# Five of six attentions make their probabilities with keys on partitions

## The reference

```python
# L0: three residual parts
x += attn(ln(x), ln(x), causal, 16 heads, rotary q and k)      # "L0s", 128 keys
x += attn(ln(x), ctx, 16 heads, rotary q and k)                # "L0c", 77 keys
x += gelu(ln(x) @ fc1 + b) @ fc2 + b
# L1
x += attn(ln(x), ln(x), 16 heads)                              # "L1s", 128 keys
x += attn(ln(x), ln(ctx), 16 heads)                            # "L1c", 77 keys
x += top-2 of 8 experts, each 128 -> 512 -> 128
# L2
x += mamba2 block(x)
x += attn(ln(x), ctx, 8 heads, mask over keys)                 # "L2c", 77 keys
# L3
x = ln(x + attn(x, ctx, 16 heads, mask over query-key pairs))  # "L3c", 77 keys
# every attention: softmax(q k^T / sqrt(width)) v, then @ wo
```

## Time and profile before

| what | value |
|---|---|
| median of 3 runs | 3726.12 us (3721.3 to 3736.9) |
| the profiled execution's own time | 3734.74 us |
| its span, first to last instruction | 3732.9 us |
| PE busy | 3195.7 us, 86% |
| ACT busy | 2652.3 us, 71% |
| DVE busy | 2605.4 us, 70% |
| POOL busy | 1246.9 us, 33% |
| mean granted clock of TensorE | 0.952 of full speed |

### The profile page before, as it was taken

One profiled execution on the slowest core, in us unless ns is written; L12 is line 12 of the kernel. 1 busy time (PEld: TensorE's weight loads), 2 busy tenths in 40 slices (PEclk: granted clock), 3 DMA queues, 4 the chain that ended last, 5 costly groups with the idle time before them and its releaser, 6 DMA issues.

```text
span 3732.9 us, 87645 instructions
## 1 busy us (share of the span) xinstructions
PE 3195.7 (86%) x30064; PEld 2269.6 (61%) x30064; DVE 2605.4 (70%) x5408; ACT 2652.3 (71%) x5088; POOL 1246.9 (33%) x1615
## 2 busy tenths in 40 slices
PE   6898888888888979998988888998888997777897
PEld 3566556566756657665665656666565665665565
DVE  7877787755477777556888777665888877326775
ACT  4777777777876757887776766788776776656566
POOL 3122333212153353112244244212235434214632
PEclk9999999999999989999999999999999998989899
DMA  7013200134410033221000014322000004442000
GB/s 280 1 43 135 109 6 15 30 97 108 103 37 3 18 100 89 69 64 43 19 22 14 3 44 109 83 72 57 26 23 20 6 19 108 103 112 59 16 2 13
DMA packets 211920, 212.98 MB, mean 57 GB/s; under 512 B 51808, under 2 KB 155168, under 8 KB 211232
## 3 DMA queue, kind: packets, MB, share of 16 engines
q1 hardware_dynamic: 203296, 190.58, 18.1%
q0 software_dynamic: 8192, 16.79, 1.5%
HBM read 135.98 MB, written 71.30 MB: 56 GB/s over the span
## 4 chain that ended last, share of the span: by engine, by line
PE 39%; DVE 23%; ACT 15%; issue 8%; SPq 7%; DMA 4%; POOL 4%; ACTq 0%; DVEq 0%; POOLq 0%
PE ps L1933 8%; DVE mx L2320 6%; PE ps L1923 5%; PE ps L1945 4%; DVE pr L2326 4%; DMA b_up<-cols 4%; ACT block_hid L2211 3%; ACT pt L2164 3%; PE ps L1892 3%; PE ps L1953 2%; PE ps L2005 2%; PE ps L1918 2%; DVE kx L2326 2%; ACT xh L2114 2%; SPq L1818 1%
## 5 line engine op out<-in xcount | busy, mean ns | idle before, releaser
L2320 DVE TENSOR_REDUCE mx<-ps 128x8 f32<-128x616 f32 (+1 forms) x704 | 671.4, 954 | 334.7 <-PE ps L1923 316.4
L2164 ACT ACTIVATE pt<-ps 77x512 f32<-77x512 f32 (+1 forms) x1408 | 768.9, 593 | 126.1 <-PE ps L1933 123.2
L2576 POOL TENSOR_TENSOR kx<-kT,in_tiles 128x308 f32<-128x308 f32 (+1 forms) x384 | 315.7, 822 | 830.5 <-PE ps L1923 740.0
L1933 PE MATMUL ps<-k_sb,pr 128*77 128x128 f32 (+1 forms) x3776 | 538.9, 284 | 33.9 <-ACT pr L2155 10.3
L1933 PEld LDWEIGHTS ps<-k_sb,pr 128*77 128x77 f32 (+1 forms) x3776 | 421.1, 147 | 142.2 <-issue 73.2
L1945 PE MATMUL ps<-pt,v 77*16 77x128 f32 (+2 forms) x11264 | 444.3, 278 | 29.0 <-ACT pt L2164 11.2
L2326 DVE TENSOR_TENSOR pr<-ps,mx 128x616 f32<-128x616 f32 (+1 forms) x472 | 450.3, 954 | 16.2
L2155 ACT ACTIVATE pr<-pr 128x616 f32<-128x616 f32 (+1 forms) x472 | 392.7, 840 | 75.6 <-DVE pr L2326 74.6
L2173 ACT ACTIVATE og<-ps 128x256 f32<-128x256 f32 x704 | 267.3, 381 | 236.8 <-PE ps L1945 233.6
L1923 PE MATMUL ps<-kx,qT 32*128 32x308 f32 (+2 forms) x2816 | 361.6, 547 | 42.2 <-ACT pt L2164 15.8
L1945 PEld LDWEIGHTS ps<-pt,v 77*16 77x16 f32 (+2 forms) x11264 | 251.8, 97 | 181.1 <-issue 85.1
(11 more groups left out here) (209 smaller groups left out, 5733.3 us busy)
## 6 DMA issues: line engine op xcount, KB each, us to landing
w_up<-weights SPq DMA_DIRECT2D x160, 256.0 KB
w_down<-weights SPq DMA_DIRECT2D x160, 256.0 KB
sent<-block_hid SPq DMA_DIRECT2D x42, 512.0 KB, 6.3
made<-block_hid SPq DMA_DIRECT2D x42, 512.0 KB, 6.3
block_rows<-sent SPq DMA_DIRECT2D x160, 64.0 KB
b_down<-expert_b SPq DMA_DIRECT2D x160, 64.0 KB
made<-block_out SPq DMA_DIRECT2D x160, 64.0 KB, 2.2
cT<-ctx_cols SPq DMA_DIRECT2D x32, 154.0 KB, 3.1
```

Of the source, the lines that this page charges most:

```text
L1933: i = tr(p[0:keys, j * L:(j + 1) * L], probs[s][pl.slot(unit, 3)][:, c:c + keys], ident)
L2164: go_act(pt[s][0:keys, q % 2, :], p[0:keys, :], ACT.Copy).then_inc(probsT_ready.sem, 1)
L2320: link(v_.tensor_reduce(m, tile, AX.X, ALU.max, negate=True))
L2576: tell(pool, g_.tensor_tensor(spread_keys[s][:, pl.slot(step, 2), 0:4 * keys].rearrange("p (h k) -> p h k", h=4), kT[s][:, b * keys:(b + 1 ...
```

## The change

Attentions 0 to 4 (all but L3c) are made another way, called flipped; those with 16 heads and 77 keys (L0c and L1c) are moreover flat. L3c stays as it was.

- `scores` stays, mask included, but now only for the maximum: `peak` is the DVE reduction alone. The addition from PSUM to SBUF, the exponential over it, the transposes of `turn` and their ACT copies are gone.
- `split` (POOL, four small instructions) writes the negated maxima as a sum of three bfloat16 numbers into `pieces`, 32 columns to a group of four heads. `shift` (PE, then a DVE copy) turns that into rows on partitions with one bfloat16 matmul.
- `scores_t` (PE) makes the scores again, transposed: the spread keys are stationary, 128 (or the keys of one head) columns at a time, the queries move. Per block of 128 queries and per row group there is one float32 matmul, and one bfloat16 matmul of a constant times the shift rows adds the maximum. For 128 keys that is four blocks x four row groups x two matmuls; for flat, the 4 x 77 = 308 keys of four heads are cut into three chunks of 128 rows, so three blocks; for the 8-head attention four blocks x two row groups. The causal mask is added again by four bfloat16 matmuls of 512 columns.
- `exp` (ACT) takes the exponential straight from two PSUM banks into SBUF, keys already on partitions: 1024 columns, or 768 for flat. The key mask of L2c is the bias of this instruction.
- `mix` is as before for 128 keys and for the 8 heads, without the wait for a copy. For flat it takes three chunks x four groups of heads, with values laid out in rows of the chunks, and ACT copies 384 columns once instead of 256 twice. `regroup` then turns three blocks instead of four and takes six DVE instructions instead of two, as heads cut by a chunk's edge come in two parts.
- Flat values need `blank` (ACT, two instructions that lay zeros and ones) and `chunk` (SP, six small transfers from the values to their rows), once per pass and attention. A third buffer for spread keys.
- `rope` has one projection into one bank, and four DVE instructions (the swap of halves is a shuffle across partitions).
- Costs, priorities and so the order of all steps on all engines are new.

```diff
+        self.flat = flip and heads == 16 and keys == LC
+        self.spreads = 3 if flip else 2
+        self.pitch = 4 * keys if self.flat else 4 * L
...
+              "L0_sa_bo", rope=True, mask="causal", norm=0, flip=True),
...
+    Attention("L2c", 8, LC, "L2_wq", "L2_wk", "L2_wv", "L2_wo", mask="keys", norm=8, flip=True),
...
+    if t.flat:
+        values = [("blank", a, s)] + values + [("chunk", a, s)]
...
+def flipped_steps(a, s):
+
+    t = ATT[a]
+    out = [("spread", a, s, 0)]
+    turned = t.halves - 1 if t.flat else 0
+    for n in range(NB + 2):
+        if n < NB:
+            out.append(("scores", a, s, n))
+            if n + 1 < NB:
+                out.append(("spread", a, s, n + 1))
+            out += [("peak", a, s, n, h) for h in range(t.halves)]
+        if 1 <= n <= NB:
+            out.append(("shift", a, s, n - 1))
+        if n < NB:
+            out.append(("split", a, s, n))
+        if n >= 3:
+            out.append(("regroup", a, s, n - 3))
+        if n >= 2:
+            out.append(("mix", a, s, n - 2, turned))
+        if 1 <= n <= NB:
+            out.append(("scores_t", a, s, n - 1))
+            out += [("exp", a, s, n - 1, h) for h in range(t.halves)]
+        if n >= 2 and t.halves == 2 and not t.flat:
+            out.append(("mix", a, s, n - 2, 1))
+    return out
...
+def last_use(a, s, b):
+
+    t = ATT[a]
+    if b >= t.spreads:
+        return ("scores_t" if t.flip else "scores", a, s, b - t.spreads)
+    return ("mix", a - 1, s, NB - 1, ATT[a - 1].halves - 1)
...
-    return TWO if step[0] == "rope" else ONE if step[0] in WITH_PSUM else None
+    return ONE if step[0] in WITH_PSUM else None
...
+        flipped = Ring([(pr[s][:, 0, :], pr[s][:, 1, :], flat_pt[s]) for s in range(S)])
...
+        def probs_by_key(s, t, slot):
+
+            if t.flat and slot < 2:
+                return flat_pr[s][:, slot * 6 * L:(slot + 1) * 6 * L]
+            return flipped[s][slot][:, 0:(6 if t.flat else 8) * L]
...
+                elif kind == "chunk":
+
+                    a, s = step[1:]
+                    sp.wait_ge(*blanked(a, s))
+                    sp.wait_ge(*values_ready(a, s))
+                    for c in range(3):
+                        for slot, (j, key, row, n) in enumerate(pieces_of_chunk(c)):
+                            sp.dma_start(value_rows(s, c)[row:row + n, slot * ROW:slot * ROW + 128],
+                                         flat_v1[s][key:key + n, j * 128:(j + 1) * 128]).then_inc(chunks_in[s], 16)
...
-                    if t.rope:
-                        i = mm(bank(pl, step, 1)[:, 0:n], W(w + "r"), src[:, 0:n], start=True, stop=True)
...
+                elif kind == "shift":
+
+                    a, s, b = args
+                    pe.wait_ge(*peaks_split(a, s, b))
+                    mm(p[:, 0:L], pieces[:, s % S, :], ident16, start=True, stop=True).then_inc(shift_turned.sem, 1)
+                elif kind == "scores_t":
+
+                    a, s, b = args
+                    t, keys = of_attention(a)
+                    pe.wait_ge(*shift_ready(a, s, b))
+                    tiles = t.heads // 4
+                    high = 128 // tiles
+                    masked = t.mask in ("causal", "pairs")
+                    if masked and t.flat:
+                        for c in range(3):
+                            lo, n = c * 128, min(128, 4 * keys - c * 128)
+                            for g in range(tiles):
+                                mm(bank(pl, step, g)[0:n, lo:lo + L], mp16[s][:, b, lo % keys:lo % keys + n], ident16, start=True, stop=False)
+                    elif masked:
+                        mask = causal16 if t.mask == "causal" else mp16[s][:, b, 0:LC]
+                        for g in range(tiles):
+                            mm(bank(pl, step, g)[0:keys, :].rearrange("p (h q) -> p h q", h=4), mask,
+                               ident16.unsqueeze(1).broadcast_to([128, 4, L]), start=True, stop=False)
+                    each = 128 if t.flat else keys
+                    for lo in range(0, 4 * keys, each):
+                        n, c = min(each, 4 * keys - lo), lo // each * L
+                        for g in range(tiles):
+                            r = slice(high * g, high * (g + 1))
+                            mm(bank(pl, step, g)[0:n, c:c + L], spread_keys(s, t, b)[r, lo:lo + n], qT[s][r, b * L:(b + 1) * L],
+                               start=not masked, stop=False)
+                        for g in range(tiles):
+                            r = slice(high * g, high * g + 32)
+                            own = fours16[r, lo:lo + n] if t.keys == LC else in_fours16[r, lo // L:lo // L + 1].broadcast_to([32, L])
+                            i = mm(bank(pl, step, g)[0:n, c:c + L], own, shifts(s, t)[r, :], start=False,
+                                   stop=not masked or t.flat or lo + n == 4 * keys)
+                    i.then_inc(scores_turned.sem, 1)
...
+                    if t.flat:
+                        pe.wait_ge(chunks_in[s], 6 * 16 * (pl.rank["chunk", a, s] + 1))
+                        for half in range(2):
+                            pe.wait_ge(*probs_ready(a, s, b, half))
+                        mine = [probs_by_key(s, t, pl.slot(("exp", a, s, b, half), 3)) for half in range(2)]
+                        for c in range(3):
+                            n = min(128, 4 * keys - c * 128)
+                            for g in range(4):
+                                at = (g % 2 * 3 + c) * L
+                                i = mm(ps[32 * g:32 * g + 32, pl.banks[step][0], c * L:(c + 1) * L],
+                                       value_rows(s, c).rearrange("p (w n) -> p w n", n=16)[0:n, :, g * NB + b],
+                                       mine[g // 2][0:n, at:at + L], start=True, stop=True)
+                        i.then_inc(mixed.sem, 1)
+                        continue
...
+                    for q in range(3 if t.flat else t.quads):
...
+                elif kind == "exp":
+                    a, s, b, h = args
+                    t, keys = of_attention(a)
+                    act.wait_ge(*scores_turned(a, s, b))
+                    old = pl.earlier(step, 3)
+                    if old:
+                        act.wait_ge(*mixed(*old[1:4], 1 if ATT[old[1]].flat else old[4]))
+                    lo = pl.banks["scores_t", a, s, b][2 * h]
+                    wide, high = (3 * L, 128) if t.flat else (4 * L, keys)
+                    dst = probs_by_key(s, t, pl.slot(step, 3))[0:high, :].rearrange("p (c x) -> p c x", c=2)
+                    src = ps[0:high, lo:lo + 2, 0:wide]
+                    if t.mask == "keys":
+                        i = go_act(dst, src, ACT.Exp, scale=t.scale, bias=mk_col[0:keys, :])
+                    else:
+                        i = go_act(dst, src, ACT.Exp, scale=t.scale)
+                    i.then_inc(probs_ready.sem, 1)
...
+                    if t.flat:
+                        go_act(og[:, s % S, 0:3 * L], p[:, 0:3 * L], ACT.Copy).then_inc(gathered.sem, 1)
...
+                elif kind == "blank":
+
+                    a, s = args
+                    if s < S:
+                        act.wait_ge(blanks_in, 6 * 16)
+                    act.wait_ge(*mixed(a - 1, s, NB - 1, ATT[a - 1].halves - 1))
+                    go_act(flat_kx[s][:, FLAT_V:FLAT_V + 59 * 16].rearrange("p (w n) -> p w n", n=16),
+                           blanks[:, 0:59].unsqueeze(2).broadcast_to([128, 59, 16]), ACT.Copy)
+                    go_act(value_rows(s, 2).rearrange("p (w n) -> p w n", n=16),
+                           blanks[:, 59:91].unsqueeze(2).broadcast_to([128, 32, 16]), ACT.Copy).then_inc(blanked.sem, 1)
...
-                    link(v_.scalar_tensor_tensor(by_batch(dst[:]), by_batch(p), C(bias), table("cos"), ALU.add, ALU.mult))
-                    link(v_.scalar_tensor_tensor(by_batch(tmp[:]), by_batch(bank(pl, step, 1)), C(bias + "r"), table("sin"),
-                                                 ALU.add, ALU.mult))
-                    tell(dve, v_.tensor_tensor(dst[:, 0:NB * m], dst[:, 0:NB * m], tmp[:, 0:NB * m], ALU.add),
+                    link(v_.scalar_tensor_tensor(by_batch(tmp[:]), by_batch(p), C(bias), table("sin"), ALU.add, ALU.mult))
+                    v_.scalar_tensor_tensor(by_batch(dst[:]), by_batch(p), C(bias), table("cos"), ALU.add, ALU.mult)
+                    link(v_.stream_shuffle(tmp[:, 0:NB * m], tmp[:, 0:NB * m], SWAP))
+                    tell(dve, v_.tensor_tensor(dst[:, 0:NB * m], dst[:, 0:NB * m], tmp[:, 0:NB * m], ALU.subtract),
...
+                elif kind == "peak":
+                    a, s, b, h = args
+                    t, keys = of_attention(a)
+                    dve.wait_ge(*scores_made(a, s, b))
+                    old = pl.earlier(("spread", a, s, b), 1)
+                    if old and ATT[old[1]].flip:
+                        dve.wait_ge(*peaks_split(*old[1:]))
```

(54 more changed lines are left out.)

1859 lines of the change are left out of this document (1039 added, 820 removed).

## The result

The changed kernel takes 4001.15 us (median of 4 runs, 3998.71 to 4019.93) beside 3726.4 (median of 4) for the kernel before, measured with it: ratio 1.074, interval 1.071 to 1.078. It is 7.4% slower; forecast were 6% less.

A forecast was written before the change was run, and what follows sets the result against it. PE, busy 86%, was taken as nearest to a bound. From 3734.7 us, PE's work -168, idle time -100 and late `shift` +30 gave 3497, scaled to about 3490 us, 6% less; range 3290 to 3700 us.

The forecast's parts named there:

- PE's work: On PE, removed transposes (-593 us) and rope projection (-52) against added `scores_t` (+418) and smaller terms: -168 us in sum.
- 8-head term: `scores_t` in L2c: 1.39 us a batch, 64 batches, with only two row groups to overlap.
- flat terms: L0c and L1c on PE: `scores_t` 1.10 us a batch, `mix` 0.84 us, 128 batches.
- ACT and DVE: Copies of `turn` leave ACT and additions leave DVE: -612 us to about 2040, and -343 us to about 2260.
- POOL: `split` adds four linked instructions 320 times, 1.2 to 1.9 us each: +480 us of POOL's queue, covered by its waiting time.
- From work to time: PE's work -168 us, a quarter of its 429 us scattered idle time -100, late `shift` +30: 3497, scaled to about 3490 us.
- Idle time going: Rival, chance 0.17: 270 of PE's 429 us of scattered idle time go, about 3300 us.
- Loads alternating with streams: Rival, chance 0.15: in `scores_t` loads don't hide behind streams within a row group, 2.2 us for 128 keys, about 3700 us.
- POOL stalling PE: Rival, chance 0.09: PE, working in order, waits for each `split` on POOL, 1.3 us a batch, about 3875 us.
- What would show it: Signs after: PE busy near 3030 us, ACT 2040, DVE 2260, shift-copy waits under 50; wrong if `scores_t` takes over 2 us.

The follow-up runs named there:

- after: The changed kernel itself, all five attentions flipped, in its own order, against the kernel before: 4001.15 us, ratio 1.074.
- three_fit: Changed kernel with only L0c, L1s and L1c flipped and the order of steps fitted anew, against the kernel before: ratio 1.024.
- bench: All five flipped, plainly ordered, with nine stretches of 40 units on PE alone put ahead of the first step: 0.45 to 2.22 us a unit.
- np_fit: All five flipped, scores made once without maxima or second group, a fixed shift, order fitted anew, against the kernel before: ratio 0.861.

## Why the prediction was wrong, point by point

- **PE's work: right in direction, half as large.** `scores_t` for 128 keys took 1.49 (forecast 1.47), the mask 0.97 (0.96), flat 1.24 (1.10), eight heads 2.22 (1.39), flat `mix` 0.98 (0.84). Over the batches 128 x 1.49 + 128 x 1.24 + 64 x 2.22 = 492 instead of 418 us, and 18 more for `mix`: -168 becomes about -76. The 8-head term is off not for lack of overlap but for the change of tile height, and the flat terms for a lesser form of it: each change to the last chunk and back costs `scores_t` some 0.1 us, and flat `mix`, which goes from 128 to 52 rows, pays 0.11 us. The trace confirms the sum: with each window of 5 us weighed by its clock, PE's work at full clock is 3058 us before and 2986 after, -72.
- **ACT and DVE: right; POOL: too dear.** ACT -544 (forecast -612), DVE -364 (-343). POOL's busy time rose by 269 us. Its four small instructions take 0.20 to 0.22 us each and start 0.28 us apart, 1.06 us in its queue for a batch, 340 us in all, below the forecast (+480) and its lower bound of 1.2 us. It cost the forecast nothing.
- **From work to time: this step failed.** It took a quarter off PE's idle time because DVE and ACT would be freer. They were, and PE's idle time rose by 170 us. It also priced all work at full clock. With PE idle more often the clock stood low for 776 us instead of 358. By the windows above PE lost 138 us of busy time to the clock before and 305 after, +167. Together -72 + 167 + 170 = +265, and the spans differ by 266. Idle time and the clock go together: in `after` the clock left full speed 87 times, and in the 5 us ahead of that PE was busy for 69%, in windows at full clock for 85%.
- **Why the idle time rose.** 4 to 5 of the 7.4 points were the order: the list of steps is fixed ahead from a table of costs, and its fit was worth about 11% before and 4% after. That costs, priorities and the order are new was known from the change, and the prediction gave it no term. Refitted, the flipped form still stands 3.8% over the refitted unflipped one, whose 1.5% under the kernel before makes up the difference. That rest isn't the chain over POOL (1 point), nor PE's sum (`three_fit`, on the other sort of chip). The second set of scores holds PSUM banks a second time, which the prediction cost at nothing; that was not tried by itself. PE's waits for what frees these banks are part of the 209 us after and 212 before, so no growth of idle time shows there; between the refitted forms (250 and 296 us) they may have part. What makes up the rest, the banks, another trait of the form or the luck of one fitted list, stays open.
- **The rivals.** Idle time going: the opposite. Loads alternating with streams: its 2.2 us fell, the step took 1.49; its mechanism stays open, as said. POOL stalling PE: 12.5 us behind `pieces`, 40 us behind all of POOL's work. That rival had the right sign by a mechanism that isn't there. None of them had the order or the clock in it.
- **What would show it.** PE busy was to be near 3030 and was 3291, a sign named in advance; so was a `scores_t` of over 2 us, and the 8-head one took 2.22. ACT (2109, forecast 2040), DVE (2242, 2260) and waits behind the shift (16 us, under 50) came about as forecast, and said nothing of the time.

## What to carry to other kernels

Where several streams share an in-order engine by a list fitted in advance, a change of form has two prices, the work and the fit that it throws away: compare both forms under one plain order (here even) and both refitted (here 12% and 9% better than plain), best with more than one fitted list each, before calling either faster. Slack on other engines is no time gained on the one that sets the end, and where its clock falls with idle time, as in these runs, idle time costs more than itself (167 us beside 170). If a change makes something twice, try the version without the first making early: with its maxima and shifts 826 us hung on it here, under the plain order.

## What the runs showed of the hardware

- Matmuls alternating between tiles of 64 and of 32 rows lose 0.13 us at each change (`bench`); with zero rows added to make both 64 high, a unit fell from 2.22 to 1.16 us. Going from 128 to 52 stationary columns, or back, cost about 0.1 us too.
- Four row groups, each with a 77-column load and a 128-column stream, run at 28 ns a float32 record (0.90 us for 32). With 128-column loads, in the kernel, a block of eight float32 and four bfloat16 records comes every 0.33 us, 28 ns a record; with 77 columns every 0.29.
- The granted clock read 1.00 from 15.4 to 386 us of short tiled matmuls without a wait for another engine. In whole kernels it was lower the more PE stood idle, on the whole: on sort A 0.952 at 14% idle, 0.913 at 17%, 0.903 at 18%; on sort B 0.919 at 16%, 0.890 at 17%, 0.878 at 20% and 22%, 0.862 at 22%, but `np_fit` had 0.895 at 21%.
- The same kernel before took 3726 us on some chips and 3880 us on others, with a clock of 0.95 and 0.93, so only ratios of one chip are set side by side, and the value of the 8-head repair stays open for that reason too.
